# The narrow heads' groups of weighted values in pairs: 2 steps per block where there were 4, with a new step order

## The reference

```python
# layer 0 (rotary embedding) and layer 2: 16 heads of 64
q = _heads(xq @ wq); k, v = _heads(ctx @ wk), _heads(ctx @ wv)
a = softmax(einsum('bhnd,bhmd->bhnm', q, k) * DH ** -0.5)
o = einsum('bhnm,bhmd->bhnd', a, v)                       # then @ wo + bo
# layers 1 and 3: 16 heads of 8 (the narrow heads)
sim = einsum('bhid,bhjd->bhij', q, k) * HD ** -0.5
out = einsum('bhij,bhjd->bhid', softmax(sim), v)          # then @ W_proj + b_proj
# every block: x = x + [gate *] block(modulate(layernorm(x), shift, scale))
```

## Time and profile before

| | |
|---|---|
| median of 3 runs | 1555.07 us (1554.9 to 1555.74) |
| the profiled execution's own time | 1554.27 us |
| its span, first to last instruction | 1552.5 us |
| mean granted TensorE clock | 0.988 |
| busy in that span | PE 1422.2, DVE 1370.8, ACT 1074.9, POOL 911.3 us |

### The profile page before, as it was taken

How to read it: one execution, slowest core, us unless ns; L and a number is a source line. 1 busy time by engine, 2 the same in 40 slices (tenths; PEclk the granted TensorE clock), 3 DMA queues, 4 the chain that set the end, 5 groups by cost and what they waited for, 6 DMA issues and landing times.

```text
span 1552.5 us, 40878 instructions
## 1 busy us (share of the span) xinstructions
PE 1422.2 (92%) x15228; PEld 1182.5 (76%) x15228; DVE 1370.8 (88%) x3745; ACT 1074.9 (69%) x4751; POOL 911.3 (59%) x1028
## 2 busy tenths in 40 slices
PE   5999989999898999899999899998999999999977
PEld 5788867778777777777878787776888877788755
DVE  5977888889999999798899999989888999998987
ACT  0577787866775685878768568467787887867753
POOL 3875664554566676556456556666755664644553
PEclk9999999999999999999999999999999999999988
DMA  9300000000000000000000000000000000000000
GB/s 314 91 2 2 2 1 2 2 2 1 6 8 4 7 6 3 2 1 2 1 8 2 7 6 3 8 6 10 2 2 2 2 2 2 3 2 2 3 3 6
DMA packets 14437, 20.91 MB, mean 13 GB/s; under 512 B 4064, under 2 KB 10784, under 8 KB 14240
## 3 DMA queue, kind: packets, MB, share of 16 engines
q1 hardware_dynamic: 14240, 18.31, 3.7%
HBM read 17.25 MB, written 1.05 MB: 12 GB/s over the span
## 4 chain that ended last, share of the span: by engine, by line
PE 52%; DVE 34%; ACT 11%; POOL 1%; issue 1%; DMA 0%; SPq 0%; ACTq 0%
PE ps L684 12%; ACT E L885 9%; DVE negmax L1140 9%; PE ps L798 8%; DVE E L1241 6%; PE ps L699 5%; PE ps L837 5%; PE ps L824 5%; PE ps L708 3%; PE ps L761 3%; PE ps L847 2%; PE ps L775 2%; DVE xn L1100 2%; PE ps L788 2%; PE ps L811 1%; DVE E L1193 1%
## 5 line engine op out<-in xcount | busy, mean ns | idle before, releaser
L885 ACT ACTIVATE E<-ps,negmax 128x128 f32<-128x128 f32 x2048 | 720.2, 420 | 165.7 <-DVE negmax L1140 159.1
L992 POOL TENSOR_TENSOR E<-E,rinv 128x512 f32<-128x512 f32 x512 | 525.0, 1042 | 263.4 <-DVE rinv L1149 261.3
L885 ACT ACTIVATION_READ_ACCUMULATOR E<-ps,negmax 128x1 f32 x2048 | 528.2, 261 | 0.0
L1140 DVE TENSOR_REDUCE negmax<-ps 128x4 f32<-128x512 f32 x512 | 324.6, 679 | 29.0 <-PE ps L761 15.4
L798 PE MATMUL ps<-consts,E 128*128 128x128 f32 x2048 | 297.5, 280 | 28.4 <-POOL E L992 14.7
L1241 DVE COPY E<-ps 128x512 f32<-128x512 f32 x448 | 297.6, 679 | 24.9 <-PE ps L798 23.4
L798 PEld LDWEIGHTS ps<-consts,E 128*128 128x128 f32 x2048 | 233.4, 143 | 82.3 <-POOL E L992 51.7
L985 POOL TENSOR_TENSOR E<-E,prod 128x512 f32<-128x512 f32 x128 | 162.2, 1274 | 67.6 <-DVE prod L1196 63.1
L894 ACT ACTIVATE VV<-ps 128x512 f32<-128x512 f32 x128 | 77.0, 619 | 173.6 <-PE ps L699 173.4
L940 POOL TENSOR_TENSOR rstd<-ve,consts 128x1 f32<-128x1 f32 (+1 forms) x192 | 108.5, 566 | 98.7 <-DVE ve L1093 91.0
L824 PE MATMUL ps<-E,VV 128*64 128x128 f32 x2048 | 130.1, 277 | 8.5 <-ACT E L885 4.7
(11 more groups left out here) (130 smaller groups left out, 2671.5 us busy)
## 6 DMA issues: line engine op xcount, KB each, us to landing
w_f<-res_f SPq DMA_DIRECT2D x6, 256.0 KB, 12.7
E<-in_x SPq DMA_DIRECT2D x16, 64.0 KB, 1.9
w_wq<-res_wq SPq DMA_DIRECT2D x2, 512.0 KB, 8.3
w_wk<-res_wk SPq DMA_DIRECT2D x2, 512.0 KB, 8.8
w_wv<-res_wv SPq DMA_DIRECT2D x2, 512.0 KB, 9.4
w_wo<-res_wo SPq DMA_DIRECT2D x2, 512.0 KB, 10.1
w_cq<-res_cq SPq DMA_DIRECT2D x2, 512.0 KB, 11.2
w_co<-res_co SPq DMA_DIRECT2D x2, 512.0 KB, 14.4
```

Of the source, the lines that this page charges most:

```text
L885: last = nc.scalar.activation(E[p][:, h, :], bank(u, j * N, (j + 1) * N), ACT.Exp, bias=negmax[p][:, h:h + 1], accum_out=sums[p][:, h:h + 1])
L992: tt(e, e, rinv[p][:, T4 * g:T4 * g + T4].unsqueeze(2).broadcast_to([N, T4, N]), ALU.mult).then_inc(done[POOL], 1)
L1140: nc.vector.tensor_reduce(negmax[p][:, T4 * g:T4 * g + T4], bank(u).rearrange("p (h m) -> p h m", h=T4), AX, ALU.max, negate=True).then_in ...
```

## The change

An `MX` step now takes two groups: `MX0` the groups 0 and 1, `MX1` the groups 2 and 3. It has eight products, waits for both groups' copies, and its cost in the planner is twice the old one. The products themselves and their sum are the same.

The planner changes too. `TAIL`, one delay per engine, becomes `tail_of`, with delays by step. `heads` costs 1.15 where it had 0.67. `waits_for_port` now has `keys` (L1131) and the sums of layer 3 (L1056, L1061). All tables of ranks are other ones, so the order is another one from the first steps on.

```diff
-TAIL = {PE: 0.16, DVE: 0.08, ACTE: 0.13, POOL: 0.04}
...
-AGE = 16.8
-TURN = [0, 0, 0, 0, 0, 0, 0, 0, -3, 0, 14, 0, 0, 0, 0, 14]
-AHEAD = {"small": 5.4, "rope": 2.3}
+AGE = 16.6
+TURN = [0, 2, 5, 2, 0, 0, 0, 0, -3, 10, 22, 1, 0, -16, 0, 14]
+AHEAD = {"rope": 5.6}
...
-            add(DVE, "heads", 0.67, (PE, "RS"), empties="RS")
+            add(DVE, "heads", 1.15, (PE, "RS"), empties="RS")
...
-        if k == "small":
-            add(PE, f"MX{g}", 0.242, (e, f"PT{g}"), (DVE, "V"), *([(PE, f"MX{g - 1}")] if g else []),
-                fills=() if g else ("PV",))
+        if k == "small" and g % 2:
+            add(PE, f"MX{g // 2}", 0.484, (turns_on(b, g - 1), f"PT{g - 1}"), (e, f"PT{g}"), (DVE, "V"),
+                *([(PE, "MX0")] if g > 1 else []), fills=() if g > 1 else ("PV",))
...
+def tail_of(key):
+    engine, step, b, _ = key
+    if engine == PE:
+        if step == "PJ":
+            return 0.23
+        return 0.21 if step[0] == "O" else 0.18 if step in ("K", "Q", "RS", "PJ0", "PJ1") else 0.175 if step[:2] == "PT" else 0.165
+    if engine == ACTE:
+        return 0.175 if step[:3] == "exp" else 0.17 if step[0] == "O" or step[:2] == "PT" else 0.14
+    return 0.08 if engine == DVE else 0.04
...
-    return key[0] == DVE and key[1] in ("norm", "squares", "factors", "heads")
+    return key[0] == DVE and (key[1] in ("norm", "squares", "factors", "heads", "keys")
+                             or key[1] == "sum" and key[2] >= L3_SELF)
...
-                    r = int(step[2])
-                    for by, count in latest_first(EMPTY[UNIT[b, s, "V"]], EMPTY[UNIT[b, s, f"PT{r}"]]):
+                    i = int(step[2])
+                    for by, count in latest_first(*[EMPTY[UNIT[b, s, n]] for n in ("V", f"PT{2 * i}", f"PT{2 * i + 1}")]):
...
-                    for j in range(T4):
-                        q0 = 32 * j
-                        last = mm(ps[q0:q0 + 32, u[0], 0:N], vmask[p][:, r, q0:q0 + 32], E[p][:, T4 * r + j, :],
-                                  start=(r == 0), stop=(r == 3), tile_position=(0, q0))
+                    for r in (2 * i, 2 * i + 1):
+                        for j in range(T4):
+                            q0 = 32 * j
+                            last = mm(ps[q0:q0 + 32, u[0], 0:N], vmask[p][:, r, q0:q0 + 32], E[p][:, T4 * r + j, :],
+                                      start=(r == 0), stop=(r == 3), tile_position=(0, q0))
                     last.then_inc(done[PE], 1)
```

More of the change, by code:

```diff
@@ L75 @@
-KEEP = {
[L76 to L81, removed]
+    (POOL, "inverse", "small"): 8, (POOL, "power", "rope"): -16, (POOL, "power", "small"): -6,
@@ new lines @@
+    (POOL, "xb", "ff"): -50, (POOL, "xb", "flat"): 10, (ACTE, "O", "flat"): 60, (ACTE, "PT", "rope"): 14,
+    (ACTE, "V", "flat"): -76, (ACTE, "exp", "rope"): -46, (PE, "C", "small"): -4, (PE, "CT", "rope"): -128,
+    (PE, "G", "small"): -38, (PE, "HC", "small"): 2, (PE, "PJ", "rope"): -4, (PE, "PJ", "small"): 8,
+    (PE, "PT", "flat"): -2, (PE, "Q", "flat"): -10, (PE, "Q", "rope"): -6, (PE, "T", "flat"): -76,
+    (PE, "T", "rope"): 20, (PE, "T", "small"): 2, (PE, "V", "flat"): -2, (PE, "V", "small"): 98,
@@ new lines @@
+    (PE, "VAR", "small"): -4, (DVE, "CT", "rope"): 20, (DVE, "G", "small"): 20, (DVE, "K", "rope"): 4,
+    (DVE, "PT", "flat"): 2, (DVE, "PV", "small"): -8, (DVE, "Q", "rope"): 4, (DVE, "T", "flat"): 4,
+    (DVE, "T", "small"): 24, (DVE, "U0", "ff"): 80, (DVE, "factors", "small"): 2, (DVE, "keys", "small"): 14,
+    (DVE, "max", "flat"): 2, (DVE, "norm", "rope"): 8, (DVE, "rcp", "flat"): 4, (DVE, "rcp", "small"): 4,
+    (DVE, "sum", "ff"): -12, (DVE, "sum", "flat"): 44}
+KEEP = {
+    (PE, "C", "small"): 2, (PE, "CT", "rope"): 2, (PE, "D", "ff"): 1, (PE, "K", "flat"): 2, (PE, "K", "rope"): 2,
+    (PE, "K", "small"): 2, (PE, "MX", "small"): 1, (PE, "O", "flat"): 1, (PE, "PJ", "flat"): 1,
+    (PE, "PJ", "rope"): 1, (PE, "PJ", "small"): 2, (PE, "PT", "flat"): 2, (PE, "PT", "rope"): 2,
+    (PE, "PT", "small"): 2, (PE, "Q", "small"): 2, (PE, "RS", "small"): 2, (PE, "S", "small"): 1,
+    (PE, "T", "ff"): 1, (PE, "T", "rope"): 2, (PE, "T", "small"): 2, (PE, "U0", "ff"): 2, (PE, "U1", "ff"): 2,
+    (PE, "V", "rope"): 3, (PE, "V", "small"): 2, (PE, "VAR", "small"): 3}
@@ L188, in steps_of @@
         add(e, f"PT{g}", 0.6 if e == DVE else 0.48, (PE, f"PT{g}"), empties=f"PT{g}")
-        if k == "small":
-            add(PE, f"MX{g}", 0.242, (e, f"PT{g}"), (DVE, "V"), *([(PE, f"MX{g - 1}")] if g else []),
-                fills=() if g else ("PV",))
+        if k == "small" and g % 2:
+            add(PE, f"MX{g // 2}", 0.484, (turns_on(b, g - 1), f"PT{g - 1}"), (e, f"PT{g}"), (DVE, "V"),
+                *([(PE, "MX0")] if g > 1 else []), fills=() if g > 1 else ("PV",))
     if k == "small":
-        add(DVE, "PV", 0.24 if b in (3, 10) else 0.2, (PE, "MX3"), empties="PV")
+        add(DVE, "PV", 0.24 if b in (3, 10) else 0.2, (PE, "MX1"), empties="PV")
         add(PE, "PJ", 0.223, (DVE, "PV"), fills=("PJ",))
@@ L373, in schedule @@
         free[e] = clock.run(start, cost[key]) if e == PE else start + cost[key]
-        end[key] = free[e] + TAIL[e]
+        end[key] = free[e] + tail_of(key)
         order[e].append(key)
@@ L413 @@
 for _b, _s, _n in UNIT:
-    _last = {"PV": "MX3", "PJ": "PJ" if KIND[_b] == "small" else "PJ1"}.get(_n)
+    _last = {"PV": "MX1", "PJ": "PJ" if KIND[_b] == "small" else "PJ1"}.get(_n)
     _fill = next(_key for _key in ORDER[PE] if _key[2:] == (_b, _s) and (_key[1] == _last or _n in FILLS[_key] and not _last))
```

## The result

Medians of twenty runs of each kernel: 1559.14 us for the changed kernel (1553.2 to 1564.2) against 1555.37 for the one before (1551.12 to 1557.13). The ratio is 1.0023, its 95% interval 1.0014 to 1.0032, so it is slower by 3.6 us. The forecast was 1547. The changed kernel also spreads over 11 us where the one before spreads over 6, though its instruction lists are as fixed, and that is the first clue. The profiled execution of the changed kernel took 1562.17 us, so it is one of its slower ones (mean clock 0.978; over the twenty runs 0.981), and what its profile loses to the clock is somewhat more than the middle run loses.

A forecast was written before the change was run, and what follows sets the result against it. PE (92% busy) and DVE (88%) were taken to bound the kernel, neither alone. Terms -3.3 + 0 - 3.6 - 1 = -7.9 from 1554.27 gave 1546.4, plus 0.8 for the median: 1547 us, range 1536 to 1561.

The forecast's parts named there:

- the end of the program: From 1469 us on, three samples instead of two fill DVE better; bounds -8 to +4.3 us, taken as -1.
- the pairs' saving: Weighted values on PE: 82 runs instead of 97, at 0.22 us each, save 3.3 us.
- added wait: PE ahead of the weighted values: a pair needs two copies; between 3.8 us gained and 15.2 lost, taken as 0.
- What bounds the kernel: PE and DVE nearly full; PE's us worth up to one where PE is later, DVE's about a third.
- rival 2: Slower: at L827 pairs stall PE behind the second group's late copy; 1567 us, or 1559 if a third wait; chance 0.15.
- The steps held for POOL: DVE's keys, layer 3 sums and a third form stall behind POOL; 10.5 us lost, 34% of it gained: -3.6.
- The noise: Differences between 100 us stretches from 100 to 1500 us make a new order's time uncertain by 6 us either way.
- The signs: Checks named beforehand: PE's busy time and idle per 100 us, waits at L827, POOL stalls, DVE's last 84 us, granted clock.
- -5.8: Alternative size of the term for DVE stalls behind POOL, from the skill's port rule and POOL's busy share: 14.7 us of waits.

The follow-up runs named there:

- e7: Changed kernel with the emptying of the narrow heads' sum done twice on DVE, some 20 us more of DVE; 1576.88 us, ratio 1.0144.
- e8: Changed kernel with the first group's products of every narrow block done twice on PE, 14 us more of PE; 1565.93 us, ratio 1.0076.
- e1: Kernel before, in its old order, with its weighted values merged into pairs; 1558.27 us, ratio 1.0014.
- e2: Changed kernel's new order with each pair split into two single steps side by side; 1557.41 us, ratio 1.0015.
- e11: Changed kernel with 30 unread products (6.5 us) on PE behind 1450 us only; 1554.99 us, ratio 0.9996.
- e10: New order with single steps and 32 unread products (7 us) on PE behind 1450 us; 1551.77 us, ratio 0.9983.
- e13: As e11, with only the 21 of 128 pairs taken apart ahead of which PE idled; 1552.34 us, ratio 0.9981.
- e9: Kernel before, old order, with 38 unread products (8.3 us) on PE behind 1450 us only; 1554.44 us, ratio 0.9997.
- e12: Changed kernel with the planner's waits_for_port as before, its order made anew from the same tables; 1583.72 us, ratio 1.0185.
- e3 to e6: Unread products in PE's waits: 52 us in changed kernel, 56 in kernel before, 12 in new order with single steps, 56 products in old order; ratios 1.0141, 1.0152, 1.0026, 1.0010.

## Why the prediction was wrong

It said faster, 1547, and the kernel is slower. The step that failed is the end of the program, priced at -1 us by DVE's share alone; the runs show some 3.7 us of slowdown there. Behind it stands the pairs' saving of 3.3 us taken as time saved, with their added wait at 0, where the pairs cost 1 to 2 us. Its working, term by term:

- **What bounds the kernel.** "an us of DVE's about a third" failed: e7 found about one for one, 0.8 without the clock's share, and e8 0.6 to 0.8 for PE. A share of the chain tells on which engine the chain ran in this execution, not what happens when that engine's work changes.
- **The pairs, -3.3.** The count of 82 runs for 97 was right, and a pair alone does take 0.57 us from start to start (1505.03 to 1505.60 in the changed kernel). The price per run was somewhat high: e1, with 78 runs, has 3.1 us less of PE's busy time and not 4.2. That it is time saved was wrong. Taken alone the pairs cost 2.2 us (e1), or 1.3 (changed kernel less e2) and 2.0 (e11 less e10); only the first is clear of noise, and all three point the same way.
- **The added wait, 0.** This is where the sign of the pairs' term was lost. The prediction weighed whether more steps wait, and took today's 9.8 us. It did not see that a step that waits now has 0.22 us more behind the wait. Of rival 2 the mechanism and the place were right in the new order (e13); its price was far too high, 11.7 us of waits and not 25. In the old order, where the pairs' cost in time is clear, only 1.8 of 7.5 us more idle time stand ahead of the weighted values, so there its way is not shown.
- **The steps held for POOL, -3.6.** Failed: the sums are longer than before. DVE's 10 us less come from steps that the planner held for POOL before as well: the two forms of `norm` at L1116, 71.3 us for 80.2 at L1100, and two operations of `heads`, L1141 with L1142, 14.9 for 20.8, in which the prediction saw no term. At e7's price those 10 us would have been worth 8 to 10; the new order by itself shows -2.2 us with the end's clock held (e10 less e9), and that within the noise.
- **The end, -1.** This is the step that decided. That three samples fill DVE better is right when the clock holds: 72.9 of 84 us in e11. Without it DVE was busy 67.7 us, 81% as before. But the same three bring PE a thin stretch of short steps in block 9, and the clock falls for 17 us on end. The prediction had the granted clock of both stretches in its rows (0.87 and 0.85) and priced the end by DVE's share alone; "a lower granted clock" stood only among the things that would prove it wrong. Fillers at the end are worth 4.2 us in the changed kernel and 0.5 in the one before: 3.7 us, give or take 2.4, which is the size of the slowdown. The products add work and change nothing else, so the higher clock is the only gain in them that the record shows.
- **The noise, 6 us either way,** was taken from how stretches of one order differ. e12 shows that an order can be off by 25.
- **The signs.** PE idles 7.0 us per 100 in the middle, as before; DVE's last 84 us are at 81%; the waits, 11.7 us, lie between the two bounds. But the clock is lower in several stretches of the middle, and the prediction had said that this would make its reasoning wrong whatever the number.

Together: the pairs +2.0 (e11 less e10), the new order -2.2 (e10 less e9), the end without fillers against the old one's +3.7. These are steps from one kernel to the next, so they add up to the measured +3.6 by themselves; the sum is no test of them, and of the three only the last is clear of noise. What stays open is how much the longer half-clock time in the middle (34 us for 17) costs: the products that e3 to e6 put there did not pay for themselves, and nothing else was tried.

The Trainium skill's rule on the shared port pair ("SBUF — State Buffer") agrees with single instructions here, with the 1.07 us of the earlier trace rows and up to 1.27 us for one of these sums in the changed kernel. As a forecast of time it gave -5.8, further off than the rows' -3.6.

## What to carry to other kernels

Joining two steps saves what lies between them and puts the first half behind the wait for both operands. Here 21 of 128 pairs carried all of the added wait, so look first which steps the profile shows waiting, and leave those apart. Price a new order by the granted clock too: the same idle time in longer lumps went with a lower clock here. Filling such waits with unread products paid at the end of the new order, where PE idles a quarter of the time; it did not at the end of the old one, nor in the middle of either. To know what an engine's time is worth, add some and measure, at the same clock; its share of the chain said a third where the answer was 0.8 to 1.

## What the runs showed that I had not expected

A kernel whose lists are fixed took 1553.2 to 1564.2 us, following its mean granted clock (0.987 to 0.978). Adding 6.5 us of useless matmuls made it 4.2 us faster. Changing one line of a planner's rules, with its tables kept, made it 25 us slower. The same kind of products, put at the end of the old order, raised its clock by as much and brought 0.5 us, which is nothing within the noise.
